# A fused non-local block, attention and top-2 expert kernel: first expert weights prepared in the head, two buffers for the first unit's maxima

## What is computed

```python
# 1. non-local block over the 1024 pixels of an image
f = softmax(theta(x)^T phi(x) / 8);  x = x + proj(f applied to x)
# 2. tokens = pixels of x; attention over the 1024 tokens of an image
n = layernorm(t);  t = t + softmax((n Wq + bq)(n Wk + bk)^T / sqrt(128)) (n Wv + bv)
# 3. top-2 of 8 experts for each of the 4096 tokens
n = layernorm(t);  w, e = top2(n Wg + bg)
t = t + sum over the two: w * (gelu(n W1[e] + b1[e]) W2[e] + b2[e])
```

## Time and profile before

| | us |
|---|---|
| median of 3 runs | 491.48 (490.86 to 491.91) |
| the profiled execution's own time | 489.35 |
| its span in the trace | 487.6 |
| PE busy | 389.0 |
| DVE busy | 370.3 |
| ACT busy | 335.2 |
| POOL busy | 313.0 |

### The profile page before, as it was taken

How to read it: one execution, slowest core, us unless ns; L and a number is a source line. 1 busy time by engine, 2 the same in 40 slices (tenths; PEclk the granted TensorE clock), 3 DMA queues, 4 the chain that set the end, 5 groups by cost and what they waited for, 6 DMA issues and landing times.

```text
span 487.6 us, 12633 instructions
## 1 busy us (share of the span) xinstructions
PE 389.0 (80%) x3948; PEld 291.9 (60%) x3949; DVE 370.3 (76%) x1012; ACT 335.2 (69%) x636; POOL 313.0 (64%) x309
## 2 busy tenths in 40 slices
PE   2666669999988799989987876658989999999552
PEld 1433337666665466666655644646879898989321
DVE  2577989998897787889898588667976666666863
ACT  3635887778785499876756875558778787888320
POOL 9200132755699856598857857767777777777780
PEclk9988999999998999999999989778999999999955
DMA  6750000610000000000510101133355333334717
GB/s 216 169 93 0 1 0 3 151 25 3 1 1 0 2 1 1 1 1 2 137 38 12 31 27 40 51 88 94 91 127 132 105 101 93 98 94 113 225 49 258
DMA packets 43836, 32.62 MB, mean 67 GB/s; under 512 B 17686, under 2 KB 36905, under 8 KB 43785
## 3 DMA queue, kind: packets, MB, share of 16 engines
q1 hardware_dynamic: 39242, 22.59, 19.0%
q0 software_dynamic: 4544, 9.38, 5.8%
HBM read 18.33 MB, written 13.60 MB: 65 GB/s over the span
## 4 chain that ended last, share of the span: by engine, by line
PE 41%; DVE 31%; ACT 10%; issue 8%; POOL 6%; DMA 2%; SPq 1%; ACTq 0%; POOLq 0%; DVEq 0%
PE MX L696 13%; PE PV L696 11%; PE SC L696 11%; DVE mx L1519 6%; DVE EL L1542 5%; PE PR L696 4%; POOL ybuf L685 3%; ACT EH L1168 2%; ACT E L1167 2%; ACT QK L1076 2%; DVE QK L1493 2%; DVE EH L1738 1%; ACT X L1076 1%; PE PR L965 1%; DVE TOK L1561 1%
## 5 line engine op out<-in xcount | busy, mean ns | idle before, releaser
L1167 ACT ACTIVATE E<-SC 128x512 f32<-128x512 f32 x128 | 77.2, 603 | 43.4 <-PE SC L696 36.5
L696 PE MATMUL PV<-VH,EH 128*128 128x129 f16 x512 | 96.0, 227 | 3.0 <-DVE TOK L1561 3.0
L696 PE MATMUL SC<-QK 128*128 128x512 f16 x320 | 90.6, 389 | 8.2 <-ACT EH L1168 6.1
L618 POOL TENSOR_TENSOR EL<-E,EH 128x1024 f32 (+1 forms) x28 | 59.6, 2128 | 56.7 <-ACT EH L1168 56.7
L696 PE MATMUL PV<-VH,EL 128*128 128x129 f16 x512 | 95.6, 225 | 0.0
L696 PE MATMUL PV<-VL,EH 128*128 128x128 f16 x512 | 95.6, 223 | 0.0
L1519 DVE TENSOR_REDUCE mx<-MX 128x1 f32<-128x1024 f32 x64 | 78.0, 1219 | 18.8 <-PE MX L696 18.5
L685 POOL DMA_INDIRECT ybuf<-EL,yid x62 | 70.0, 1130 | 18.9 <-issue 17.4
L569 POOL DMA_INDIRECT zbuf<-ZZ,posi x64 | 66.4, 1038 | 21.3 <-issue 18.2
L1168 ACT ACTIVATE EH<-SC 128x512 f32 (+1 forms) x128 | 77.6, 606 | 0.0
L696 PE MATMUL MX<-QK,EH 128*128 x624 | 62.2, 246 | 1.9 <-DVE EL L1749 1.9
(11 more groups left out here) (231 smaller groups left out, 886.8 us busy)
## 6 DMA issues: line engine op xcount, KB each, us to landing
EH<-zbuf SPq DMA_DIRECT2D x39, 130.0 KB, 2.4
X<-in_x_dram SPq DMA_DIRECT2D x4, 512.0 KB, 5.1
zbuf<-zer SPq DMA_DIRECT2D x16, 128.0 KB, 4.0
X<-in_L_ffn_W_dram SPq DMA_DIRECT2D x1, 2048.0 KB
EL<-ybuf SPq DMA_DIRECT2D x4, 512.0 KB, 4.2
out_dram<-X SPq DMA_DIRECT2D x8, 256.0 KB, 4.8
W1H<-in_L_ffn_W_dram SPq DMA_DIRECT2D x4, 256.0 KB
W1L<-in_L_ffn_W_dram SPq DMA_DIRECT2D x4, 256.0 KB
```

The costliest lines, as they stand in the source:

```text
L618: nc.gpsimd.tensor_tensor(EL[:, w % 2, ds(i * 2, 2), c], E32h[1], EH[:, w % 2, ds(i * 2, 2), c], ALU.subtract).then_inc(e32_free[1], 1)
L696: return nc.tensor.matmul(o, w, r, start=start, stop=stop)
L1167: nc.scalar.activation(E32h[h][:, p, :], SC[:, p, :], ACT.Exp, scale=sc)
```

## The change

It does the following.

- W1 is loaded by SP right after the small weights, into `EL1` (read as float32, called `W1w`); the eight row-0 broadcasts go into `EH1`, to partitions 1 to 127 only; DVE clears partition 0 of these two halves with two 1x2048 memsets. b1 follows when W1 has landed.
- POOL does the subtraction of row 0 and the low halves at the end of its setup list, ahead of step 0. ACT's `first_weights(i)` stands at the end of each pair of step -1, and waits for POOL's piece i.
- DVE waits for the low halves ahead of the work of step 1, PE ahead of the first expert tile.
- The DMAs that fill unused `zbuf` tiles are issued after unit 0's rows. W2 is loaded in SP's unit 2, to X.
- In step -1 the maxima of even tiles go to `SC` (`first_maxima`), those of odd tiles to `MX`.
- In steps -2 and -1 ACT makes `X16h` before it copies `TOK`.

The core of the diff:

```diff
-        W10b = [t[:].bitcast(F32) for t in (W1H, W1L)]
+        W10b = [EH1[:, h * PAIRS * S:(h + 1) * PAIRS * S].bitcast(F32) for h in range(2)]
+        W1w = EL1.bitcast(F32)
+        first_maxima = (WIDE[0], MX[:])
@@ sync
             sp.dma_start(Wg0b[:], Wg[0, :].partition_broadcast(P)).then_inc(g_in, 16)
+            sp.dma_start(W1w.rearrange("p (e h) -> p e h", e=E), W1.rearrange("e d h -> d e h")).then_inc(w1_in, 16)
+            for e in range(E):
+                sp.dma_start(W10b[e // PAIRS][1:P, e % PAIRS * HID:(e % PAIRS + 1) * HID],
+                             W1[e, 0, :].partition_broadcast(P - 1)).then_inc(w1_row_in, 16)
             sp.wait_ge(b_in, 16 * 6)
...
-            for e in range(E):
-                sp.dma_start(W10b[e // PAIRS][:, e % PAIRS * HID:(e % PAIRS + 1) * HID],
-                             W1[e, 0, :].partition_broadcast(P)).then_inc(w1_in, 16)
...
+            sp.wait_ge(w1_in, 16)
+            sp.dma_start(W1w[0:1], b1).then_inc(w1_in, 16)
...
                 row(m, 1)
+                if m == 0:
+                    unused_tiles()
@@ gpsimd
+            pool.wait_ge(w1_zeroed, 2)
+            pool.wait_ge(w1_row_in, 16 * E)
+            pool.wait_ge(w1_in, 32)
+            for i in range(PAIRS):
+                c = slice(i * S, (i + 1) * S)
+                nc.gpsimd.tensor_tensor(W1w[:, c], W1w[:, c], W10b[i // 2][:, i % 2 * S:(i % 2 + 1) * S],
+                                        ALU.subtract).then_inc(w1_augmented, 1)
+            for i in range(PAIRS):
+                pool.wait_ge(wexp_scaled, i + 1)
+                c = slice(i * S, (i + 1) * S)
+                nc.gpsimd.tensor_tensor(W1L[:, c], W1w[:, c], W1H[:, c], ALU.subtract).then_inc(wexp_lo, 1)
@@ tensor
+                    if s == -1:
+                        pe.wait_ge(mx_free, i * 2 + (n_mx + p) if p else i * 2 + n_mx)
+                    else:
+                        pe.wait_ge(mx_free, i * 2 + (n_mx + p + 1))
+                    o_ = first_maxima[p] if s == -1 else MX
...
+                    if first and u == 0:
+                        pe.wait_ge(mx_free, n_mx)
@@ scalar
-                if s == 4:
-                    act.wait_ge(w1_augmented, PAIRS)
                 def first_weights(i):
+                    act.wait_ge(w1_augmented, i + 1)
                     c = ds(i * S, S)
-                    cp(W1H[:, c], Xw[:, c], svec[:, 1:2])
-                    cp(Xw[:, c], Xw[:, c], svec[:, 1:2]).then_inc(wexp_scaled, 1)
+                    cp(W1H[:, c], W1w[:, c], svec[:, 1:2])
+                    cp(W1w[:, c], W1w[:, c], svec[:, 1:2]).then_inc(wexp_scaled, 1)
...
-                    if s == 4:
+                    if s == -1:
                         first_weights(i)
@@ vector
+            nc.vector.memset(W10b[0][0:1], 0.0).then_inc(w1_zeroed, 1)
             dve.wait_ge(w_hi, 1)
...
+            nc.vector.memset(W10b[1][0:1], 0.0).then_inc(w1_zeroed, 1)
```

More of the change, by code:

```diff
@@ L418, in _, with unused_tiles @@
             sp.dma_start(Wg32[0:1, :], bg).then_inc(g_in, 16)
-            for e in range(E):
-                sp.dma_start(W10b[e // PAIRS][:, e % PAIRS * HID:(e % PAIRS + 1) * HID],
-                             W1[e, 0, :].partition_broadcast(P)).then_inc(w1_in, 16)
[L423 to L427, removed]
             for r in (0, 32):
                 sp.dma_start(B232[r:r + E, :], b2).then_inc(b2_in, 16)
+            sp.wait_ge(w1_in, 16)
+            sp.dma_start(W1w[0:1], b1).then_inc(w1_in, 16)
+            def unused_tiles():
+                sp.wait_ge(iotas, 7)
+                unused = zbuf[E * CAP:, :].rearrange("(n q p) r -> n p q r", q=2, p=P)
+                for n in range(E):
+                    sp.dma_start(unused[n, :, :, 0:2 * P], zer[:]).then_inc(pad_static, 16)
+                    sp.dma_start(unused[n, :, :, 2 * P:ROW], padid[:, E + n].bitcast(F16)).then_inc(pad_static, 16)
             def row(m, h):
@@ L765, in maxima @@
                 def maxima(i, p):
[L767 removed]
+                    if s == -1:
[3 more added lines that the diff above has]
+                    o_ = first_maxima[p] if s == -1 else MX
                     for h in range(2):
[L769 removed]
+                        last = mm(o_[:, h * HALF:(h + 1) * HALF], QH[:, slot(m), ds(i * 256 + p * P, P)],
                                   KH[:, slot(m), h * HALF:(h + 1) * HALF], True, True)
@@ L1185, in pair @@
                     if first and v is not None and v < B:
-                        residual_stream()
-                        high_x()
+                        if s < 0:
+                            high_x()
+                            residual_stream()
+                        else:
+                            residual_stream()
+                            high_x()
                     if v is not None and B <= v < UNITS:
@@ L1518, in maxima @@
                     t = i * 2 + p
-                    nc.vector.reduce_max(mx[:, t:t + 1], MX[:], AX.X).then_inc(mx_free, 1)
+                    if s == -1 and t == 0:
+                        dve.wait_ge(mx_free, n_mx + 1)
+                    nc.vector.reduce_max(mx[:, t:t + 1], first_maxima[p] if s == -1 else MX[:], AX.X).then_inc(mx_free, 1)
                 def scaled(h):
```

42 lines of the change are left out of this document (8 added, 34 removed).

## The result

The changed kernel takes **558.77 us** (median of 4, 558.19 to 559.11) where before takes 491.17 in the same set of runs (489.6 to 491.91). The ratio is 1.1408, interval 1.1366 to 1.1449: 67.6 us slower. The profiled execution took 559.07 us, with a span of 557.1 and a mean granted clock of 0.87. The prediction said 563 us and a range of 546 to 610. Executions of one kernel differ; every ratio here is taken from those within about 1.5% of that kernel's fastest, and the profiles of e4, e9 and e10 are of slower executions (493.40, 549.43 and 556.03 us), which matters where their times are compared.

The account below looks back on a forecast made before the run. No engine was full over the whole span (PE busiest, 80%); DVE set step -1's pace. Step 0 81.5 us later, less 8.5 in later steps, gave +73 us: 564.5 against the median, rounded down to 563, range 546 to 610.

Parts of the forecast that it names:

- One engine for the 127 rows: Head: all eight 127-row copies run on the same single DMA engine, 87 us, from 17.5 to 104.5; chance 0.76.
- the sign that the prediction named: Head: DMA share of about 0.06 and 24 GB/s from some 18 to 105 us, with PE, DVE and ACT idle.
- The price of a packet: Row copies: one engine takes 85.4 ns for each 2 KB packet, 24 GB/s, so 1016 packets take 87 us.
- The 72 us for the copies: Row copies: side estimate from the skill page's 27 GiB/s an engine, putting the time at about 549 us.
- The other end of the range: Row copies: one engine but slower, 9.4 GB/s, 220 us instead of 87, time 696 us; chance 0.10.
- b1 behind the row copies: Head: b1 follows the row copies on the same engine, taking 3.8 us, to 108.3.
- From POOL's first piece to step 0's tokens: Head: from POOL's first piece at 110.7 to the end of the tokens' high half at 126.9, 16.2 us.
- The head's own gains: Tokens split about 2 us sooner in step -2, 1 in step -1, each pair's idle 1 us gone; all swallowed.
- the spread case: Head: row copies spread over the engines all the same; with faster copies the head gains up to 5 us; chance 0.14.
- Steps 3 to 6: Later steps, relieved of W1's work: step 3 gives back 7.0 us, step 4 0.8, step 5 0.7; total 8.5.
- The rival on the other side: Head: copies spread all the same, POOL's first piece at 34.7, minus 3 us in all, time 488.5 us; chance 0.14.
- The sum: Whole kernel: step 0 81.5 us later, minus 8.5 in the later steps, +73 us on the profiled execution.

Follow-up runs that it names:

- e4: Before with only the two head edits (two buffers for the first maxima, tokens split before TOK is copied); no ratio, times 483.97 and 492.81 to 493.94 us.
- e9: e6 with W1 loaded into partitions 1 to 127 only and b1 sent to partition 0 ahead of it; ratio 0.9674.
- e10: e8 plus the zbuf fill issued behind the first unit's rows; ratio 0.9774, medians 552.19 us against 556.72 for before.
- e1: The changed kernel with row copies to all 128 partitions, POOL zeroing partition 0 behind them; 485.58 us, ratio 0.9936.
- e2: The changed kernel with each 127-row copy cut into 112 and 15 rows; 483.43 us, ratio 0.9886.
- e5: The changed kernel with each 127-row copy cut into 124 and 3 rows; ratio 1.0164.
- e3: Before with only its eight row-0 copies changed, to 127 rows (partitions 1 to 127); 564.79 us, ratio 1.1555.
- e8: The same kernel as e4, before with only the two head edits, in another set; ratio 1.0115.
- e7: e2 without the head edits: one buffer for the first maxima and the old token order; ratio 1.0025.
- e6: e2 with W1's load and row copies in pieces of two experts with own semaphores, b1 in four parts behind; 548.62 us, ratio 0.9847.
- e12: e9 run once more, unchanged, in a later set; 475.73 us, ratio 0.9793.
- e11: e9 without POOL's four subtractions for W1's low half, W1L zeroed ahead instead; 475.70 us, ratio 0.9778.

## Why the prediction was right, point by point

- **One engine for the 127 rows**: right. The share of 0.07 at 25 GB/s from 30 to 90 us is the sign that the prediction named; e1 and e2 take the loss away by the number of rows alone, e5 puts a fourth of the engines to work, and e3 makes the loss in the kernel before.
- **The price of a packet**: 85.4 ns by the earlier trace rows, measured 82.0 (one copy holds SP for 10.42 us, 127 packets). One engine alone was a little quicker, as I had guessed, by 4%: the 1016 packets take 83.3 us and not 87. The 72 us for the copies that stand beside the prediction's sum are too low; the price from the earlier trace rows was the better one. The other end of the range, 9.4 GB/s an engine from the earlier trace rows, was no end: that rate belongs to the mixture at 14 to 20 us, not to a single engine.
- **b1 behind the row copies**: right in kind. POOL's wait ends at 104.3 us with b1's landing, where I had 108.3. The terms are off in both directions. The row copies end at 102.3 us, where I had 104.5: the packets took 3.7 us less, but the copies began about 1.5 us later, at about 19.0. And b1 cost 2.0 us (102.3 to 104.3), not 3.8. I took 3.77 us from its one packet in before as the time of one engine for 16 KB; the same packet took 0.61 us in after, e2 and e5. One packet seen once was no sound price.
- **From POOL's first piece to step 0's tokens**: 106.6 (end of the first piece) to 124.06 is 17.4 us, for which I had 16.2. The term was 1.2 us too small. I had let ACT run through without a wait; its rows have waits for PE of 0.25, 0.65 and 0.25 us in the last two pairs. PE's granted clock was 0.50 from 109 to 121 us, and six matmuls of a projection took 0.80 us there where they took 0.49 in before. The sum had no term for the clock after the long stop. That the clock makes these waits is argued from the rows; no run holds it apart. Sum of the head: +78.7 against +81.5.
- **The head's own gains**: "all swallowed" holds for after. What I had as up to 5 us in the spread case is about 9 for the unit itself (e8), of which before's order of issues would let nothing through, and W1's work leaves 2.4.
- **Steps 0 and 1**: I had nothing, it was +1.1 us. No run tells why.
- **Steps 3 to 6**: 7.38, 1.53, 0.96 and 0.59 against 7.0, 0.8, 0.7 and 0. The term mis-sized is steps 4 and on: together they gave 3.1 us, not 1.5, and the gain reached step 6. I put this down to ACT's and POOL's relief; no run takes the two apart. The stop of the earlier trace rows is gone, and step 3 (29.41) is the like of step 2 (29.80), as the prediction took it.
- **The rival on the other side** had 488.5 us for spread copies, 3 us under before. e2 is 5.1 us under before in its set: the direction was right, and POOL's start 3.7 us too late, almost all of it b1's packet.
- **The sum**: of spans I had +73, measured 69.5. The head was 2.8 us too large and the later steps 2.0 too small, and 1.3 us of losses (steps 0 and 1, behind step 7) were missing. So part of the closeness is errors that cancel: 4.0 us too much up to POOL's start against 1.2 too little behind it.

## What to carry to other kernels

Before a copy goes into a queue whose number of rows isn't a multiple of sixteen, look for the divisors of that number: eight copies of 127 rows took 83 us, cut in 112 and 15 rows some 9 (about 19 to 27.9 us in e2), and nothing in the code looks different. A copy that is off the critical path is not free either; ask what is issued behind it on the same engine, because both the fill of zbuf (e8) and the slow rows (e3) did their harm to a transfer of 256 bytes. And when an engine's idle time is taken away, find first which hidden wait stands under it: here the head edits gave their 8 us (e10) only after the line of SP was changed.

## What the runs showed of the hardware that I had not expected

- A queue of slow transfers holds its issuer. SP, which had issued W1's load in 0.43 us and the first row copy in 0.49, stood 10.42 us at each of seven issues in a row behind them in after, the length of one whole copy, and the last of the seven is a bias of 0.5 KB (81.71 us). In e3 it is 10.4 to 10.6 us each, and the last of them is the first transfer of the zbuf fill (80.25 us).
- The time of one packet is not a constant: b1's 16 KB took 3.77 us in before and 3.85 in e3, 1.85 in e1, 0.73 in e7 and 0.61 in after, e2 and e5. Why stays open.
- Order in the queue can matter more than size: in e6 four packets of 4 KB for b1, issued from 20.2 us on, released POOL at 28.9.
- Beside POOL's subtractions of 128x1024 a DVE operation of 0.23 us took 2.07, about the length of one of POOL's (2.12). The subtraction of the tokens' low half, 1.23 us by itself, took 3.13 us in e9, and 2.67 in e12 and 2.25 in e11, both begun while POOL's first piece ran; the maxima of 1.22 us, which read PSUM, kept their time beside POOL (e12, 31 to 37 us).
- With the engines idle for some 80 us the granted clock stood at 0.50, the lower level. In e2 it falls between 29 and 30 us, with PE still from 26.7 to 34.2, stands at 0.50 until 42, and six matmuls of a projection take 0.80 us at 34.23, where they take 0.51 at 23.95 in the same run, at 1.00.
